# Four-block decoder kernel: who computes the layer norm that ends the mixture, VectorE or GpSimd

## The chip, the core and the metric

One core of one Trainium2 chip. The metric is the device time of one execution in microseconds (us). Engines are named as the profile names them: PE (TensorE, matrix products), DVE (VectorE), ACT (ScalarE), POOL (GpSimd), SP (SyncE, which only issues transfers here).

## What is computed

A decoder of two layers over x of 4 batches x 512 tokens x 128 channels. Each of its six steps is `x = layernorm(x + step(x))`. Cut to the two steps that matter here:

```python
# step 3: mixture of 16 experts, top 2, and a shared expert
hidden = silu(x @ gate) * (x @ up)            # per expert
x = layernorm(x + combine(hidden @ down) + shared(x))

# step 4: delta rule, 16 heads of 64
# W_t = W_(t-1) + beta_t (v_t - W_(t-1) k_t) k_t^T,   o_t = W_t q_t
x = layernorm(x + o @ Wout)

def layernorm(x): m = mean(x); v = mean((x - m)**2); return (x - m) / sqrt(v + 1e-5)
```

## The kernel before

x stays in SBUF as `X`, 16 tiles of 128 tokens x 128 channels, and is worked on in four blocks (one batch each, `xb(b)`, 128 partitions x 512 float32). Its transpose is `XT`. The stages are lettered: B is cross-attention, C the mixture, D the delta rule. Each engine runs its own instruction list in program order. `weave` mixes several generators into that list at build time: a `yield` is a point where another stream's instructions may come in. What stands in a list stays in that order whatever happens on the chip, and a wait at the head of an engine's list holds all that stands behind it.

Mixture (C). `c_experts_*` runs nine pairs of experts for each block: PE computes gate and up, ACT the silu (line 1318), DVE multiplies (lines 1335 and 1341, both with one operand in PSUM). Each block's turn also carries three side streams: the router of the next block (whose last DVE step, lines 1273 and 1275, writes `c_CT`, which PE needs before it can weight the next block's experts), the down projection of the block before, and that block's norm. `c_down_vector` adds the four down-projected tiles into `X` (line 1361) and then calls `normalize(..., "xr_C", fine=True)`: a sum per token (line 191), the mean (193), `x - mean` in place (197), the square into the one scratch tile `sq` (200), its sum (204), the variance (207), an inverse root by bit trick and three Newton steps in instructions of four elements per partition (lines 174, 176, 180, 165), and the product `x * root` (213), which raises `xr_C`. PE then transposes the block (`turn_tensor`, line 221). The norms of blocks 0, 1 and 2 run inside the turns of blocks 1, 2 and 3; that of block 3 runs later, in `c_last_vector`.

Already during the turns of blocks 2 and 3, the keys of the delta rule are made ready (`d_rows_*`, `d_turn_*`, with an inverse root of their own on tiles `d_z*`, and line 1600, which scales the keys `d_KV`).

Delta rule (D). The tokens are cut in chunks, and each chunk needs the inverse of a triangular matrix. There are eight such jobs m, each worth half the heads of one batch. `d_blocks_vector` (line 1638, two transposes) hands a job to GpSimd, `d_inverse_gpsimd` does it in 62 dependent instructions (lines 1709 and 1712), `d_back_vector` (line 1646, two transposes) and `d_back_scalar` bring it back as `d_XE`. PE multiplies with `d_XE` first in `corner`, then ACT negates (`d_NW`), DVE transposes a tile (`d_X`, line 1908), and PE runs `fold`. In `c_order`, the call `run(back(lane, 0))` stands right behind the mixture's weave: on DVE, all of block 3's adds and norm, the next job's transposes and everything of stage D stand behind its wait for the inverse of job 0.

GpSimd's list around the change: `d_clear_gpsimd` (a memset); `d_split_gpsimd` (line 1461, low halves of three weight matrices, each waiting for ACT); then the eight inverses; then four bias additions of the last stage.

Of the kernel before, what the change touches and what calls it, by code (L numbers as in the profile page):

```python
# [10 lines left out]
ALU = mybir.AluOpType  # L11
ACT = mybir.ActivationFunctionType
AX = mybir.AxisListType.X

NB, T, D, TC = 4, 512, 128, 154
# [13 lines left out]
    "f_lt": ("a_mz", 1), "f_lg": ("a_vz", 4), "f_oh": ("a_out", 4), "f_ctp": ("a_add", 4), "f_m": ("a_on", 16),  # L29
    "f_bm": ("a_oc", 16), "f_xm": ("a_pv", 64),  # L30
    "d_inv": ("a_ws", 4), "d_x1": ("b_kv", 6), "d_btm": ("b_kt", 6), "xr_E": ("xr_A", 4), "xr_F": ("xr_B", 4), "f_wh": ("d_wh", 3),
}


# [28 lines left out]
def run(gen):  # L63
    for _ in gen:
        pass


def bc(a, n):
    return a.unsqueeze(2).broadcast_to([a.shape[0], a.shape[1], n])
# [56 lines left out]
def build(nc, io, phases=6):  # L126
    with ExitStack() as ctx:
        sems = {}

        def sem(name):  # L130
            name = SHARED.get(name, (name, 0))[0]
            if name not in sems:
                sems[name] = ctx.enter_context(nc.semaphore(name))
            return sems[name]
# [3 lines left out]
        def at(name, shape, dt, word):  # L138
            return nc.alloc_sbuf_tensor_at(name, shape, dt, offset=SB0 + 4 * word)
# [6 lines left out]
        sq = at("sq", [128, 4, 128], F32, 4416)  # L146
        st = at("st", [128, 14, 4], F32, 4928)
# [4 lines left out]
        def xb(b):  # L152
            return X[:, 4 * b:4 * b + 4, :]
# [10 lines left out]
        def stt(e, out, a, s, b, op0, op1):  # L164
            return e.scalar_tensor_tensor(out=out, in0=a, scalar=s, in1=b, op0=op0, op1=op1)  # L165
# [4 lines left out]
        def rsqrt_steps(v, x, y, a, b):  # L170

            e = v.e
            v.wait_own()
            e.tensor_scalar(a.bitcast(I32), x.bitcast(I32), 1, None, ALU.logical_shift_right).then_inc(*v.step())
            v.wait_own()
            e.tensor_scalar(y.bitcast(I32), a.bitcast(I32), -1.0, float(MAGIC), ALU.mult, ALU.add).then_inc(*v.step())
            for k in range(3):
                yield
                v.wait_own()
                e.tensor_tensor(a, y, y, ALU.mult).then_inc(*v.step())  # L180
                v.wait_own()
                stt(e, b, a, -0.5, x, ALU.mult, ALU.mult).then_inc(*v.step())
                yield
                v.wait_own()
                stt(e, y, b, 1.5, y, ALU.add, ALU.mult).then_inc(*v.step())

        def normalize(v, x, eps, done=None, out=None, k=0, fine=False):

            e = v.e
            out = x if out is None else out  # L190
            e.tensor_reduce(st[:, k, :], x, AX, ALU.add).then_inc(*v.step())  # L191
            v.wait_own()
            e.tensor_scalar(st[:, k + 1, :], st[:, k, :], 1.0 / D, None, ALU.mult).then_inc(*v.step())
            if fine:
                yield
            v.wait_own()
            e.tensor_tensor(out, x, bc(st[:, k + 1, :], D), ALU.subtract).then_inc(*v.step())  # L197
            yield
            v.wait_own()
            e.tensor_tensor(sq[:], out, out, ALU.mult).then_inc(*v.step())  # L200
            if fine:
                yield
            v.wait_own()
            e.tensor_reduce(st[:, k + 2, :], sq[:], AX, ALU.add).then_inc(*v.step())
            yield
            v.wait_own()
            e.tensor_scalar(st[:, k + 3, :], st[:, k + 2, :], 1.0 / D, eps, ALU.mult, ALU.add).then_inc(*v.step())
            for _ in rsqrt_steps(v, st[:, k + 3, :], st[:, k + 4, :], st[:, k + 5, :], st[:, k + 6, :]):
                if fine:
                    yield  # L210
            yield
            v.wait_own()
            last = e.tensor_tensor(out, out, bc(st[:, k + 4, :], D), ALU.mult)  # L213
            if done:
                last.then_inc(sem(done), 1)
            else:
                last.then_inc(*v.step())
# [381 lines left out]
        def a_gpsimd(p):  # L599
            a_clear_gpsimd(p)  # L600
            for G in range(NG):
                a_row_gpsimd(p, G)
                if G in (0, 1, 4, 8):
                    a_split_gpsimd(p, (0, 1, 4, 8).index(G))
                if G % 4 == 2:
                    a_bias_gpsimd(p, G // 4)
# [530 lines left out]
        def b_gpsimd(p):  # L1137
            for u in range(NU):
                for s in range(11):
                    b_low_gpsimd(p, u, s)  # L1140
# [215 lines left out]
        def c_down_vector(v, b):  # L1356
            v.wait_ge("xr_B", b + 1)
            v.wait_ge("xt_B", b + 1)
            for n in range(4 * b, 4 * b + 4):
                v.wait_ge("c_dm", n + 1)  # L1360
                v.e.tensor_tensor(X[:, n, :], X[:, n, :], PS[:, bank["cd", n], 0:128], ALU.add).then_inc(sem("c_add"), 1)
                if n % 4 < 3:
                    yield
            v.wait_ge("c_add", 4 * b + 4)
            yield from normalize(v, xb(b), 1e-5, "xr_C", fine=True)

        def c_order(lane, route, experts, tail, rows, turn, last, blocks, back, split, parts):

# [81 lines left out]
        def d_clear_gpsimd(p):  # L1450

            p.wait_ge("b_sc", 11 * NU)
            p.wait_ge("b_mt", 16 * NU)
            p.wait_ge("b_r", 96 * NU)
            p.wait_ge("b_mr", 16 * NU)
            p.e.memset(d_XB, 0.0).then_inc(sem("d_zv"), 1)

        def d_split_gpsimd(p):
            for k, (w, f) in enumerate(((d_wk, d_fk), (d_wq, d_fq), (d_wv, d_fv))):
                p.wait_ge("d_wh", k + 1)  # L1460
                p.e.tensor_tensor(w[:, 1], f, w[:, 0], ALU.subtract).then_inc(sem("d_wl"), 1)
# [237 lines left out]
        def d_inverse_gpsimd(p, m):  # L1699
            e, G, XI = p.e, d_G[m % 2], d_XI[m % 2]  # L1700
            p.wait_ge(f"d_gr{m % 2}", 16 * (m // 2 + 1))
            p.wait_ge("d_gt", 2 * m + 2)
            for t in range(31, 0, -1):
                n = 32 - t
                tm = d_tmp[:, 0:t * n].rearrange("p (s t) -> p s t", s=t)
                a = G[:, t, 0:t].unsqueeze(2).broadcast_to([128, t, n])
                x = XI[:, t, t:32].unsqueeze(1).broadcast_to([128, t, n])
                p.wait_own()
                e.tensor_tensor(tm, a, x, ALU.mult).then_inc(*p.step())  # L1709
                p.wait_own()  # L1710
                z = XI[:, 0:t, t:32]
                last = e.tensor_tensor(z, z, tm, ALU.subtract)  # L1712
                if t > 1:
                    last.then_inc(*p.step())
            last.then_inc(sem("d_inv"), 1)
# [360 lines left out]
        def c_last_vector(v):  # L2076
            end = c_down_vector(v, NB - 1)
            for _ in range(3):
                next(end)
            yield from end  # L2080
# [433 lines left out]
        def none(lane, *_):  # L2514
            return iter(())
# [3 lines left out]
        @block.tensor  # L2519
        def _(e):  # L2520
            t = Lane(e, sem, "pe")
            a_tensor(t)
            b_tensor(t)
            if phases == 2:
                run(b_tail_tensor(t))
                return
            c_order(t, c_route_tensor, c_experts_tensor, b_tail_tensor(t), lambda t, m: d_rows_tensor(t, m, ring),
                    lambda t, m: d_turn_tensor(t, m, ring), c_down_tensor, lambda t: later(3, ()), none, lambda t: later(3, ()), lambda t, b: later(2, ()))
            hidden = f_hidden_tensor(t, 0)
            d_order(t, d_chain_tensor, d_prep_tensor, lambda t, m: d_keys(t, d_rows_tensor, d_turn_tensor, m, ringD),  # L2530
                    lambda t, m: d_rows_tensor(t, m, ringD), lambda t, m: d_turn_tensor(t, m, ringD), d_late_tensor, e_first_tensor,
                    e_attend_tensor, none, c_last_tensor, none, none, lambda t, b: f_route_tensor(t, b, ringD), hidden, none)
            f_start_tensor(t)
            f_order(t, f_hidden_tensor, hidden, f_route_tensor, none, f_late_tensor)
# [33 lines left out]
        @block.gpsimd  # L2568
        def _(e):
            p = Lane(e, sem, "pool")  # L2570
            a_gpsimd(p)
            b_gpsimd(p)
            if phases == 2:
                return
            d_clear_gpsimd(p)
            d_split_gpsimd(p)
            for m in range(NH):
                d_inverse_gpsimd(p, m)
            for b in range(NB):
                f_bias_gpsimd(p, b)  # L2580
# [124 lines left out]
```

## Time and profile before

| | us |
|---|---|
| median of 3 runs | 1770.7 (1767.85 to 1774.16) |
| the profiled execution | 1774.49 |
| its span in the profile | 1772.7 |
| norms of mixture blocks 0, 1, 2 on DVE (sum to product) | 1010.80 to 1027.42, 1054.52 to 1072.70, 1106.12 to 1122.13 |
| inverses of jobs 0 and 1 on POOL | 1085.05 to 1124.65, 1146.14 to 1184.58 |

All times inside the kernel count from the start of the span. A row of a timeline gives start, length, engine, line, operation, output <- inputs and, in brackets, how long the engine had been idle and what released it. A line number can be that of a helper.

### The profile page before, as it was taken

To read this page: it belongs to the slowest core of one execution; us is meant where nothing else is said; L and a number is where in the kernel's file an instruction comes from. 1 tells how busy PE (TensorE), PEld (TensorE's weight loads), DVE (VectorE), ACT (ScalarE), POOL (GpSimd) and SP (SyncE) were. 2 spreads that over 40 slices of the span, in tenths; PEclk is the share of its full clock that TensorE was granted. 3 is DMA by queue.
4 is the path that set the end of the run, shared out by engine and by line. 5 is a ranking of instruction groups with operands and counts; after the bars stand their busy time and mean duration, and the time that the engine had idled before them with its cause. 6 is when DMAs were issued, how large, how long until landed. Compare 5 with 4: busy or idle time off the path is not lost.

```text
span 1772.7 us, 41545 instructions
## 1 busy us (share of the span) xinstructions
PE 1526.5 (86%) x17916; PEld 800.5 (45%) x17916; DVE 1214.3 (68%) x2341; ACT 915.1 (52%) x1269; POOL 681.6 (38%) x716
## 2 busy tenths in 40 slices
PE   5887877789999999999988988788989899898985
PEld 1222222333334333433423544677777788665542
DVE  6889875777774776667545667766866775565776
ACT  1676654566774777577574333355445444333220
POOL 1111000355564655466473104467855567000000
PEclk9999998899999999999998998799999998879998
DMA  4000002223322222223120100000000001100000
GB/s 149 1 1 1 1 1 81 85 70 88 93 81 58 81 70 85 54 86 102 38 69 14 62 1 13 13 15 4 16 15 16 15 4 35 50 2 1 1 13 12
DMA packets 32407, 70.63 MB, mean 40 GB/s; under 512 B 5328, under 2 KB 7056, under 8 KB 31968
## 3 DMA queue, kind: packets, MB, share of 16 engines
q1 hardware_dynamic: 32224, 67.98, 13.1%
q8 instruction: 141, 2.31, 0.5%
q14 instruction: 42, 0.34, 0.1%
HBM read 47.45 MB, written 20.51 MB: 38 GB/s over the span
## 4 chain that ended last, share of the span: by engine, by line
PE 58%; DVE 28%; ACT 6%; issue 5%; DMA 1%; POOL 1%; SPq 0%; DVEq 0%; ACTq 0%; POOLq 0%
PE ps L159 56%; DVE a_MX L401 4%; DVE b_mx L834 3%; PE ps L221 1%; PE ps L1523 1%; DVE st L165 1%; DVE b_VL L781 1%; DVE sq L200 1%; DVE d_KV L1600 1%; POOL b_EL L906 1%; ACT d_L L162 1%; DVE st L191 1%; DMA b_M<-s_xq 1%; DVE X L197 1%; DVE d_zb L165 1%
## 5 line engine op out<-in xcount | busy, mean ns | idle before, releaser
L906 POOL TENSOR_TENSOR b_EL<-b_X,b_EH 128x1024 f16<-128x1024 f32 x160 | 341.2, 2133 | 309.0 <-ACT b_EH L162 309.0
L834 DVE TENSOR_REDUCE b_mx<-ps 128x2 f32<-128x666 f32 x256 | 216.9, 847 | 99.9 <-PE ps L159 99.7
L888 ACT ACTIVATE b_X<-ps 128x1024 f32<-128x1024 f32 x160 | 163.8, 1024 | 133.9 <-PE ps L159 132.9
L1709 POOL TENSOR_TENSOR d_tmp<-d_G,d_XI 128x31 f32<-128x31 f32 (+15 forms) x248 | 128.9, 520 | 193.2 <-DVE d_G L1638 174.4
L162 ACT ACTIVATE b_EH<-b_X 128x1024 f16<-128x1024 f32 x160 | 169.1, 1057 | 27.9 <-PE ps L159 16.7
L159 PE MATMUL ps<-b_M,b_S 128*128 128x512 f16 (+1 forms) x768 | 177.1, 384 | 2.0 <-ACT b_X L888 2.0
L438 ACT ACTIVATE a_E<-ps 128x1024 f32<-128x1024 f32 x128 | 131.3, 1025 | 91.0 <-PE ps L159 90.5
L401 DVE TENSOR_REDUCE a_MX<-ps 128x2 f16<-128x1024 f32 x128 | 155.4, 1226 | 29.1 <-PE ps L159 27.7
L1712 POOL TENSOR_TENSOR d_XI<-d_XI,d_tmp 128x31 f32<-128x31 f32 (+15 forms) x248 | 141.0, 569 | 19.5
L159 PE MATMUL ps<-b_Hk,b_Hq 64*128 64x333 f16 x512 | 82.6, 319 | 40.4 <-DVE b_mx L834 36.1
L420 POOL TENSOR_TENSOR a_QS<-a_QS,a_MR 128x512 f16<-128x512 f16 x16 | 18.5, 1157 | 234.7 <-ACT a_MR L162 234.7
L159 PEld LDWEIGHTS ps<-b_Hk,b_Hq 64*128 64x128 f16 x512 | 24.6, 93 | 164.1 <-DVE b_mx L834 139.5
L159 PEld LDWEIGHTS ps<-b_M,b_S 128*128 128x128 f16 (+1 forms) x768 | 55.5, 97 | 77.2 <-issue 25.2
L2446 POOL TENSOR_TENSOR f_Y<-X,f_bo 128x512 f32<-128x512 f32 x4 | 6.1, 1536 | 215.5 <-DVE X L213 112.8
L159 PE MATMUL ps<-f_XM,f_Wh 128*128 128x512 f16 x256 | 78.1, 387 | 0.0
L159 PE MATMUL ps<-a_QS,a_KS 32*128 32x512 f16 x256 | 52.2, 405 | 29.8 <-DVE a_MX L401 28.7
L162 ACT ACTIVATE d_UW<-ps 128x512 f32<-128x512 f32 x64 | 38.2, 597 | 68.9 <-PE ps L159 68.9
L159 PE MATMUL ps<-a_E,a_VA 128*32 128x512 f32 x512 | 72.9, 643 | 0.3
L159 PE MATMUL ps<-d_KV,d_XE 64*64 64x128 f32 x1024 | 72.7, 291 | 0.1
L159 PE MATMUL ps<-b_EH,b_VH 128*64 128x512 f16 x320 | 65.5, 406 | 5.0 <-POOL b_EL L906 2.5
L1318 ACT ACTIVATE c_SG<-ps 128x512 f32<-128x512 f32 x36 | 21.5, 597 | 88.1 <-PE ps L159 86.5
L159 PEld LDWEIGHTS ps<-d_KV,d_XE 64*64 64x64 f32 x1024 | 62.2, 145 | 5.2 <-issue 4.2
(322 smaller groups left out, 3324.2 us busy)
## 6 DMA issues: line engine op xcount, KB each, us to landing
b_S<-s_xk SPq DMA_DIRECT2D x48, 336.0 KB, 6.3
b_M<-s_xq SPq DMA_DIRECT2D x48, 256.0 KB, 5.0
s_xk<-b_Hk SPq DMA_DIRECT2D x16, 336.0 KB, 2.2
s_xk<-b_Lk SPq DMA_DIRECT2D x16, 336.0 KB, 2.5
s_xq<-b_Hq SPq DMA_DIRECT2D x16, 256.0 KB, 2.0
s_xq<-b_Lq SPq DMA_DIRECT2D x16, 256.0 KB, 2.0
d_XI<-eye SPq DMA_DIRECT2D x8, 512.0 KB, 3.8
f_w<-f_w SPq DMA_DIRECT2D x1, 2048.0 KB, 8.1
```

Of the source, the lines that this page charges most:

```text
L159: return e.matmul(out, lhsT, rhs, start=start, stop=stop, skip_group_check=True)
L162: return e.activation(out, a, ACT.Copy)
L165: return e.scalar_tensor_tensor(out=out, in0=a, scalar=s, in1=b, op0=op0, op1=op1)
L401: v.e.tensor_reduce(out, PS[:, bk:bk + 2, :], AX, ALU.max).then_inc(sem("a_mx"), 1)
L420: p.e.tensor_tensor(a_QS[G % 4], a_QS[G % 4], a_MR[G % 2], ALU.add).then_inc(sem("a_q2"), 1)
L438: a.e.activation(a_E[c][:, 2 * hp:2 * hp + 2, :], PS[:, bk:bk + 2, :], ACT.Exp, scale=float(D) ** -0.5).then_inc(sem("a_ex"), 1)
L834: v.e.tensor_reduce(out, PS[:, bk:bk + 2, 0:333], AX, ALU.max).then_inc(sem("b_mx"), 1)
L888: a.e.activation(b_X[k % 2], PS[:, bk:bk + 2, :], ACT.Exp, scale=0.125).then_inc(sem("b_ex"), 1)
L906: last = p.e.tensor_tensor(b_EL[k % 6], b_X[k % 2], b_EH[k % 6], ALU.subtract)
L1318: a.e.activation(c_SG[n % 3], PS[:, bank["cgu", b, p], :], ACT.Silu).then_inc(sem("c_sl"), 1)
L1709: e.tensor_tensor(tm, a, x, ALU.mult).then_inc(*p.step())
L1712: last = e.tensor_tensor(z, z, tm, ALU.subtract)
```

## The change

For blocks 0, 1 and 2, DVE keeps the two sums, the mean, the variance and the roots. The difference, the square and the last product go to GpSimd. Three semaphores pass the work: `c_nm` (mean ready), `c_nq` (squares ready), `c_ny` (root ready, by a new copy of four elements per partition). Block 3 is as before. DVE's first wait, for `c_nq`, stands ahead of the second sum. GpSimd's list becomes: memset; difference and square of block 0; the weight splits; product of block 0; block 1; block 2; and then the inverses.

```diff
             v.wait_ge("c_add", 4 * b + 4)
-            yield from normalize(v, xb(b), 1e-5, "xr_C", fine=True)
+            v.wait_ge("xr_C", b)
+            if b == NB - 1:
+                yield from normalize(v, xb(b), 1e-5, "xr_C", fine=True)
+            else:
+                yield from c_norm_vector(v, b)
+
+        def c_norm_vector(v, b):
+            e = v.e
+            e.tensor_reduce(st[:, 0, :], xb(b), AX, ALU.add).then_inc(*v.step())
+            v.wait_own()
+            e.tensor_scalar(st[:, 1, :], st[:, 0, :], 1.0 / D, None, ALU.mult).then_inc(sem("c_nm"), 1)
+            yield
+            yield
+            yield
+            v.wait_ge("c_nq", b + 1)
+            e.tensor_reduce(st[:, 2, :], sq[:], AX, ALU.add).then_inc(*v.step())
+            yield
+            v.wait_own()
+            e.tensor_scalar(st[:, 3, :], st[:, 2, :], 1.0 / D, 1e-5, ALU.mult, ALU.add).then_inc(*v.step())
+            for _ in rsqrt_steps(v, st[:, 3, :], st[:, 4, :], st[:, 5, :], st[:, 6, :]):
+                yield
+            v.wait_own()
+            e.tensor_copy(st[:, 7, :], st[:, 4, :]).then_inc(sem("c_ny"), 1)
+            yield
+
+        def c_norm_gpsimd(p, b):
+            e, x = p.e, xb(b)
+            p.wait_ge("c_nm", b + 1)
+            p.wait_ge("xt_B", b + 1)
+            e.tensor_tensor(x, x, bc(st[:, 1, :], D), ALU.subtract).then_inc(*p.step())
+            p.wait_own()
+            e.tensor_tensor(sq[:], x, x, ALU.mult).then_inc(sem("c_nq"), 1)
+            yield
+            p.wait_ge("c_ny", b + 1)
+            p.wait_ge("c_nq", b + 1)
+            e.tensor_tensor(x, x, bc(st[:, 7, :], D), ALU.mult).then_inc(sem("xr_C"), 1)
@@ gpsimd
             d_clear_gpsimd(p)
+            first = c_norm_gpsimd(p, 0)
+            next(first)
             d_split_gpsimd(p)
+            run(first)
+            for b in range(1, NB - 1):
+                run(c_norm_gpsimd(p, b))
             for m in range(NH):
                 d_inverse_gpsimd(p, m)
```

(The three semaphores are also given shared numbers in a table at the top of the file.)

## Rows read from the trace of the kernel before

**Rows 1.** Page of the profile: busy time of each engine over the span.

```profile
PE 1526.5 (86%) x17916; PEld 800.5 (45%) x17916; DVE 1214.3 (68%) x2341; ACT 915.1 (52%) x1269; POOL 681.6 (38%) x716
```

**Rows 2.** Busy by stretch: length, PE, PEld, DVE, ACT, POOL, granted clock, DMA share, GB/s.

```profile
1080.00:1122.00 42.00, 34.55 (x143) 18.24 (x141) 36.06 (x64) 14.41 (x24) 32.64 (x56) 0.92 0.04 13
1122.00:1163.00 41.00, 35.31 (x748) 31.48 (x749) 21.12 (x50) 15.63 (x25) 16.85 (x36) 0.83 0.05 15
...
1144.50:1148.00 3.50, 3.42 (x124) 3.39 (x128) 1.76 (x7) 1.18 (x2) 1.47 (x6) 0.50 0.02 7
```

**Rows 3.** Timeline of PE (start us, length us, ..., idle before it <-releaser), mixture to delta rule.

```profile
1021.58 2.07 PE L159 MATMUL ps<-XT,c_gt 128*128 128x512 f32 x2 [4.30 <-DVE c_CT L1275]
...
1066.60 2.08 PE L159 MATMUL ps<-XT,c_gt 128*128 128x512 f32 x2 [7.20 <-DVE c_CT L1275]
...
1106.14 1.61 PE L159 MATMUL ps<-XT,c_gt 128*128 128x512 f32 x2 [1.70 <-DVE X L1361]
...
1139.22 1.20 PE L159 MATMUL ps<-d_XE,d_L 32*32 32x32 f32 x64
...
1144.58 1.92 PE L159 MATMUL ps<-d_NW,d_X 32*32 32x32 f32 x64 [2.92 <-DVE d_X L1908]
```

**Rows 4.** Timeline of POOL (GpSimd), from the weight splits to the second inverse.

```profile
1014.36 2.21 POOL L1461 TENSOR_TENSOR d_wv<-d_fv,d_wv 128x1024 f16<-128x1024 f32 x1 [0.33 <-ACT d_wv L162]
1085.05 0.24 POOL L1709 TENSOR_TENSOR d_tmp<-d_G,d_XI 128x31 f32<-128x31 f32 x1 [68.48 <-DVE d_G L1638]
...
1124.40 0.25 POOL L1712 TENSOR_TENSOR d_XI<-d_XI,d_tmp 128x31 f32<-128x31 f32 x1
1146.14 0.24 POOL L1709 TENSOR_TENSOR d_tmp<-d_G,d_XI 128x31 f32<-128x31 f32 x1 [21.48 <-DVE d_G L1638]
...
1184.33 0.25 POOL L1712 TENSOR_TENSOR d_XI<-d_XI,d_tmp 128x31 f32<-128x31 f32 x1
```

**Rows 5.** Timeline of DVE (VectorE), norm of block 0.

```profile
1011.52 0.44 DVE L193 TENSOR_SCALAR st<-st 128x4 f32<-128x4 f32 x1
...
1014.62 2.50 DVE L200 TENSOR_TENSOR sq<-X 128x512 f32<-128x512 f32 x1
...
1020.85 0.68 DVE L1275 TENSOR_TENSOR c_CT<-ps,c_CT 16x512 f16<-16x512 f32 x1
```

**Rows 6.** Timeline of DVE, norm of block 2.

```profile
1121.44 0.69 DVE L213 TENSOR_TENSOR X<-X,st 128x512 f32<-128x512 f32 x1
```

**Rows 7.** Groups of DVE by line and form (xcount | busy us, mean ns), 1053 to 1069.

```profile
L165 DVE SCALAR_TENSOR_TENSOR d_zy<-d_zb,d_zy 128x64 f32<-128x64 f32 x3 | 0.7, 223 | 0.1
...
L1600 DVE TENSOR_TENSOR d_KV<-d_KV,d_f 128x512 f32<-128x512 f32 x4 | 2.6, 686 | 0.0
```

**Rows 8.** The same groups, 1093 to 1110, where POOL inverts.

```profile
L165 DVE SCALAR_TENSOR_TENSOR d_zy<-d_zb,d_zy 128x64 f32<-128x64 f32 x3 | 2.1, 696 | 0.1
...
L1600 DVE TENSOR_TENSOR d_KV<-d_KV,d_f 128x512 f32<-128x512 f32 x4 | 3.9, 1026 | 0.0
```

**Rows 9.** Groups of POOL by form, whole span: float32 tiles of 128x512.

```profile
L2446 POOL TENSOR_TENSOR f_Y<-X,f_bo 128x512 f32<-128x512 f32 x4 | 6.1, 1536 | 215.5 <-DVE X L213 112.8 <-PE ps L159 102.7
L315 POOL TENSOR_TENSOR X<-X,a_bo 128x512 f32<-128x512 f32 x4 | 5.1, 1269 | 0.0
```

**Rows 10.** Timeline of DVE, from the first inverse's use to the fold.

```profile
1129.03 2.28 DVE L1646 STREAM_TRANSPOSE d_XE<-d_XI 128x512 f32<-128x512 f32 x2
...
1141.51 1.15 DVE L1638 STREAM_TRANSPOSE d_G<-d_L 128x512 f32<-128x512 f32 x1 [0.94 <-ACT d_L L162]
...
1143.77 0.70 DVE L1908 STREAM_TRANSPOSE d_X<-d_XE 128x512 f32<-128x512 f32 x1
```

**Rows 11.** Timeline of ACT (ScalarE) in the same stretch.

```profile
1131.35 2.12 ACT L162 ACTIVATE d_XE<-d_XE 32x1024 f32<-32x1024 f32 x2 [5.63 <-DVE d_XE L1646]
1138.73 0.60 ACT L1840 ACTIVATE d_QT<-ps 128x512 f32<-128x512 f32 x1 [5.26 <-PE ps L159]
1139.36 2.12 ACT L162 ACTIVATE d_L<-d_L 32x1024 f32<-32x1024 f32 x2
```

More of the change, by code:

```diff
@@ L31 @@
     "d_inv": ("a_ws", 4), "d_x1": ("b_kv", 6), "d_btm": ("b_kt", 6), "xr_E": ("xr_A", 4), "xr_F": ("xr_B", 4), "f_wh": ("d_wh", 3),
+    "c_nm": ("b_pm", 144), "c_nq": ("b_lo", 144), "c_ny": ("b_pc", 144),
 }
```

## The prediction

> **What bounds the kernel now.** I read first the busy times: PE is busy 86% of the span, POOL 38% [rows 1]. POOL as a whole has room, so the question is only where the moved steps stand in its list. Second, the stretches around the change [rows 2]. From 1080 to 1122 DVE is busy 36.06 of 42 us and PE 34.55, and from 1122 to 1163 DVE is busy 21.12 of 41. So DVE is the tight engine in the second half of the mixture and has air right behind it. Third, PE's timeline says where DVE sets the time: PE sits idle 4.30 us ahead of 1021.58 and 7.20 us ahead of 1066.60, both until DVE has written `c_CT`, then 1.70 us ahead of 1106.14 for the last add into `X`, and 2.92 us ahead of the first fold at 1144.58 for `d_X` [rows 3]. Fourth, POOL's timeline: the inverse of job 0 runs from 1085.05 to 1124.65, that of job 1 from 1146.14 to 1184.58, each following at once on DVE's `d_G` [rows 4]. DVE takes up the first one at 1129.03 [rows 10], 4.4 us after it ended. These four views give the shape of the case: the change frees DVE where it is tight, and puts the end of block 2's norm ahead of an inverse that today runs beside it.
>
> **Block 0.** Today the mean is there at 1011.96, and the square takes 2.50 us from 1014.62 [rows 5]. It is long because the last weight split, which began at 1014.36 and took 2.21, had to end first (1016.57) [rows 4]. A 128x512 float32 pass costs POOL 1.27 us (four bias additions) to 1.54 (four others) [rows 9]. I take 1.27: those ran with nothing waited for before them, as these will. The mean comes at about 1011.7, as no split is in its way. Difference and square end at 1014.4, so DVE's second sum starts 2.7 us sooner than the end of today's square, 1017.12. But the three splits, 2.2 us each, now begin at 1014.5 and end at 1021. Behind that sum and one expert pair DVE is at 1016.4 with the small steps of the root, all with their operands in SBUF. Where POOL works without a gap, such a step takes as long as POOL's instruction: 696 ns against 223 [rows 7, 8]. So each remaining split lets one through: they end at 1021.5 in place of about 1020.1, and `c_CT`, which follows and for which PE waits, ends at 1022.8 in place of 1021.53 [rows 3, 5]. Cost +1.3 us. Bounds: -2.5, if the small steps slip in between splits, to +1.5. The Trainium skill ("SBUF — State Buffer", section "Who interferes with whom") has this as a rule: the pair of ports that VectorE and GpSimd share is locked for a whole instruction, and whoever asks later stands still. By that rule the square's 2.50 us is a wait of 1.95 and 0.55 of work, and the trace agrees. It speaks against moving passes to GpSimd beside small VectorE steps, and it is the rule behind the +1.3.
>
> **Block 1.** No split is near. DVE drops two passes of 0.69 us ahead of `c_CT`. POOL's two passes, 2.5 us together, fall on the start of the keys' root chain and hold two of its steps, up to 1.3 us. Net -0.3, bounds -1.4 and +1.3. The product on POOL instead of DVE ends about 1 us later. Its taker is the transpose of the block one turn later, and the same hand-over in block 2 lies at `c_last`, so both are covered. Blocks 0 and 1 together: +1.0 us.
>
> **Block 2: the relief.** The inverse of job 0 leaves this stretch. DVE's eleven instructions of the keys' root chain lose 0.47 us each (696 to 223 ns), at most 5.2; the four scalings of the keys 0.34 each (1026 to 686), 1.4 [rows 7, 8]; three passes move away, at least 2.1, less 0.2 for the new copy. That is 8.5 us of DVE work. PE can't use all of it: in this stretch it is idle for 42 - 34.55 = 7.45 us, and its granted clock is 0.92, worth another us or two [rows 2]. I take 8 us of relief. Bounds: 4, if PE or the wait for POOL's squares keeps half, to 9.5, PE's idle time and clock together.
>
> **Block 2: the price.** POOL's list is in order, and all of block 2's norm now stands ahead of the first inverse. The root is ready when the product starts today, 1121.44 [rows 6], less 8, plus 1.0, plus 0.1 for the copy: 1114.5. The product takes 1.3, so the inverse of job 0 begins at 1115.9 and not at 1085.05. It takes 39.60 us beside busy DVE, 38.44 for job 1 [rows 4]. DVE will stand still, so 38.4: end at 1154.3, which is 29.6 later than 1124.65.
>
> **What is late next.** DVE's list holds its wait for the inverse ahead of block 3's adds, its norm and the hand-over of job 1. PE does block 3's down projections, which need nothing of that, and then stops at `corner`. From the inverse's end to the fold every step now follows on the one before: two transposes 2.28 (one row for both) [rows 10], the copies of `d_XE` 2.12, one copy of `d_QT` 0.60, the copies of `d_L` 2.12 [rows 11], and from their end (1141.48) to the fold at 1144.58 another 3.1, in which DVE runs the rest up to `d_X` [rows 3, 10]. With hand-overs 10.4. DVE's adds and first passes of block 3 fit beside these 4.8 us of ACT. Today that way has 1144.58 - 1124.65 = 19.9 us, so 9.5 of the delay are absorbed. The fold moves to 1164.7: +20.1 us. The inverse of job 1 waits for `d_G`, of which one half stands ahead of `d_X` and the other right behind, so it moves by the same amount, and from there on all four engines are late together. I find nothing later that isn't: the loads of stage D are behind the same marks.
>
> **The sum.** +1.0 - 8 + 0.1 + 1.3 + 0.1 for the norm's end against the start of the product (1121.44), 1115.9; + 38.4 + 10.4 = 1164.7; less 1144.58 = +20.1. Against the profiled execution's 1774.5 that is 1794.6. That execution lies 3.8 above the median of the runs, so against the median, 1770.7, it is 1790.8: 1791. With the bounds (relief 4 to 9.5, blocks 0 and 1 -3.5 to +1.5, the pass 1.27 to 1.54, the inverse 38.4 to 39.6) the forecast's own range is +15 to +26: 1786 to 1797.
>
> **Rivals.** (1) PE's clock. Today PE has `corner` in hand at 1139.22 [rows 3]; 8 us sooner its work ahead of it is done, and `d_XE` comes at 1154.3 + 4.5, so PE rests from about 1131 to 1159. After only 2.92 us of idleness it ran at half clock, 1.2 GHz, from 1144.5 to 1148 [rows 2, 3]. If a longer rest keeps it at half clock for some 14 us of work more, 7 us come on top: 1798. Against it: the way to the fold is bound by ACT and DVE, and today's fold is run at half clock too. The Trainium skill ("TensorE: Matmul & The Clock Gate") says that an array that rested starts again at 1.2 GHz; here that holds for either kernel, so it changes the chance of this rival little. (2) The relief doesn't come, so that the change doesn't do what it says: DVE waits at `c_nq` for POOL's squares and for the ports, as it waited today for its own passes. Price 6 to 8 us: 1798. For it: the square of block 0, 2.50 us [rows 5]; against it: by block 2 there is nothing else in POOL's list. (3) Stage D takes some of the delay back, as PE is idle 14% of the time from 1122 to 1163 [rows 2]; a third to all but 5 us of the delay gone is 1776 to 1784. Against it: those idle times are waits for steps that are late as well. (4) The other side: the delay of the inverse is hidden. This needs the inverse to end by 1144.58 - 10.4 = 1134.2, that is the inverse to start by 1095.8, ahead of block 2's norm. Then only the relief is left, +1.0 - 8: 1764. The list of POOL forbids it, unless I misread where the norm of block 2 stands.
>
> **How the numbers follow.** Chances: forecast 0.70, (1) 0.12, (2) 0.08, (3) 0.07, (4) 0.03. The range 1781 to 1799 holds the forecast whole, most of (1) and (2) and some of (3). What a measurement can tell from no change is 0.3%, 5.3 us: faster is below 1765.4, slower above 1776.0. Faster: (4), 0.03. Same: the low edge of (3), 0.02. Slower: 0.95.
>
> **What would show it.** POOL: first inverse from about 1116 to 1154, and its idle time before it no longer ended by `d_G` but by the norm's product. DVE: idle some 25 us ahead of line 1646, released by POOL, and PE idle about as long ahead of the first `corner`. From 1092 to 1114 the keys' root steps at about 0.22 us. `c_CT` of block 0's turn near 1023, and its PE wait above 4.3 us. Wrong would be: a wait at `corner` under 15 us, small steps still at 0.6 us, or a last stretch, from fold to end, whose length has changed by more than 3 us.

## The result, and the profile after

The changed kernel takes 1791.07 us (median of 4 runs, 1786.92 to 1796.1). The kernel before took 1771.22 beside it. The ratio is 1.011, with a 95% interval of 1.0082 to 1.0138: 20 us slower. The profiled execution took 1788.91 us, and its span is on the page:

```profile
span 1786.9 us, 41557 instructions
...
PE 1515.1 (85%) x17916; PEld 793.3 (44%) x17916; DVE 1203.0 (67%) x2335; ACT 914.5 (51%) x1269; POOL 687.6 (38%) x725
```

[Rows 1] answers to it: POOL gained 6 us of work and DVE lost 11, and the kernel got slower all the same. The added line of code shifts the lines of helpers by one (159 is now 160) and those of the delta rule by 36 (1709 is now 1745).

POOL's timeline (columns as in [rows 4]) shows the new order of its list. `1395`, `1397` and `1401` are difference, square and product, `1497` a weight split:

```profile
1012.99 1.04 POOL L1395 TENSOR_TENSOR X<-X,st 128x512 f32<-128x512 f32 x1 [64.61 <-DVE st L1376]
1014.11 1.04 POOL L1397 TENSOR_TENSOR sq<-X 128x512 f32<-128x512 f32 x1
1015.11 2.13 POOL L1497 TENSOR_TENSOR d_wk<-d_fk,d_wk 128x1024 f16<-128x1024 f32 x1
1017.20 2.12 POOL L1497 TENSOR_TENSOR d_wq<-d_fq,d_wq 128x1024 f16<-128x1024 f32 x1
1019.27 2.12 POOL L1497 TENSOR_TENSOR d_wv<-d_fv,d_wv 128x1024 f16<-128x1024 f32 x1
...
1104.04 1.04 POOL L1395 TENSOR_TENSOR X<-X,st 128x512 f32<-128x512 f32 x1 [29.28 <-DVE st L1376]
1105.16 1.04 POOL L1397 TENSOR_TENSOR sq<-X 128x512 f32<-128x512 f32 x1
...
1114.81 1.04 POOL L1401 TENSOR_TENSOR X<-X,st 128x512 f32<-128x512 f32 x1 [8.61 <-DVE st L1388]
1115.81 0.24 POOL L1745 TENSOR_TENSOR d_tmp<-d_G,d_XI 128x31 f32<-128x31 f32 x1
...
1152.07 0.25 POOL L1748 TENSOR_TENSOR d_XI<-d_XI,d_tmp 128x31 f32<-128x31 f32 x1
1165.15 0.24 POOL L1745 TENSOR_TENSOR d_tmp<-d_G,d_XI 128x31 f32<-128x31 f32 x1 [12.82 <-DVE d_G L1674]
```

The reader is to see three things. A pass takes 1.04 us. The first inverse (1115.81 to 1152.32) follows on the product of block 2 without a gap, where it ran from 1085.05 to 1124.65 [rows 4]. The second starts at 1165.15, 19.0 us later than 1146.14.

DVE, norms and the first use of the inverse:

```profile
1017.39 1.95 DVE L1384 TENSOR_SCALAR st<-st 128x4 f32<-128x4 f32 x1
1019.37 2.04 DVE L175 TENSOR_SCALAR st<-st 128x4 int32<-128x4 int32 x1
...
1022.84 0.68 DVE L1276 TENSOR_TENSOR c_CT<-ps,c_CT 16x512 f16<-16x512 f32 x1
...
1105.20 2.15 DVE L1636 TENSOR_TENSOR d_KV<-d_KV,d_f 128x512 f32<-128x512 f32 x2
...
1107.88 0.67 DVE L1381 TENSOR_REDUCE st<-sq 128x4 f32<-128x512 f32 x1
...
1114.56 0.17 DVE L1388 COPY st<-st 128x4 f32<-128x4 f32 x1
...
1152.43 2.24 DVE L1682 STREAM_TRANSPOSE d_XE<-d_XI 128x512 f32<-128x512 f32 x2 [32.09 <-POOL d_XI L1748]
1154.57 0.84 DVE L1362 TENSOR_TENSOR X<-X,ps 128x128 f32<-128x128 f32 x4
```

DVE stands still for 32.09 us, released by POOL; in the kernel before it took the inverse up at 1129.03 with no wait [rows 10]. The first two rows are steps of four elements per partition that took 1.95 and 2.04 us, one beside each of the last two splits. PE, in the same two places:

```profile
1023.57 2.08 PE L160 MATMUL ps<-XT,c_gt 128*128 128x512 f32 x2 [5.06 <-DVE c_CT L1276]
...
1068.07 2.07 PE L160 MATMUL ps<-XT,c_gt 128*128 128x512 f32 x2 [5.80 <-DVE c_CT L1276]
...
1154.87 1.46 PE L160 MATMUL ps<-d_wv,d_XS 128*128 128x256 f16 x6 [27.65 <-DVE X L1362]
1156.13 1.48 PE L160 MATMUL ps<-d_XS,d_wq 128*128 128x512 f16 x3
...
1163.56 1.20 PE L160 MATMUL ps<-d_NW,d_X 32*32 32x32 f32 x64 [2.48 <-DVE d_X L1944]
```

PE waits 5.06 us for `c_CT` of block 0's turn (4.30 before) and 5.80 for that of block 1 (7.20 before) [rows 3]. Then it stands still for 27.65 us, and the fold comes at 1163.56 in place of 1144.58. The same two stretches as in [rows 2], with the first one cut where the product starts (length, PE, PEld, DVE, ACT, POOL, granted clock, DMA share, GB/s):

```profile
1080.00:1114.00 34.00, 32.20 (x143) 17.64 (x144) 26.74 (x61) 13.70 (x23) 2.08 (x2) 1.00 0.06 17
1122.00:1163.00 41.00, 11.42 (x133) 8.84 (x131) 8.40 (x17) 7.08 (x9) 26.56 (x49) 0.67 0.04 13
```

In the first stretch PE is busy 95% of the time at full clock, where it was 82% at 0.92 from 1080 to 1122. In the second, PE is busy 11.42 us of 41, against 35.31. One stretch got faster and one stood still.

**A common ruler.** Single executions start the stage some us apart (1010 to 1020 us from the start of the span). So all kernels are measured from the same start below: the last of the four adds of block 0 into `X` (line 1361 or 1362) to the start of the first fold. This way is called the ruler. The kernel before needs 134.10 us (1010.48 to 1144.58), the changed one 151.86 (1011.70 to 1163.56). That is +17.8. It is read in one execution of each kernel, so differences of a us or two on it need a row that explains them. From the fold to the end of the span they need 628.1 and 623.3, and all further kernels 620 to 624, so the kernel before had a slow tail of 4 us or more in its profiled execution. The spans differ by 1.2 + 17.8 - 4.8 = 14.2 us, the medians by 19.9.

### The profile page after: what moved, and what is told of

It is laid out like the page before. It is cut to its first block, busy times and chain, and to the rows that moved or that the text cites. A ratio compares the mean times of both kernels' runs of the same rounds, so it can differ in the third digit from the quotient of the medians.

```text
span 1786.9 us, 41557 instructions
## 1 busy us (share of the span) xinstructions
PE 1515.1 (85%) x17916; PEld 793.3 (44%) x17916; DVE 1203.0 (67%) x2335; ACT 914.5 (51%) x1269; POOL 687.6 (38%) x725
## 4 chain that ended last, share of the span: by engine, by line
PE 57%; DVE 27%; ACT 6%; issue 5%; POOL 3%; DMA 1%; SPq 0%; DVEq 0%; ACTq 0%; POOLq 0%
PE ps L160 55%; DVE a_MX L402 4%; DVE b_mx L835 3%; PE ps L222 1%; POOL d_XI L1748 1%; DVE st L166 1%; POOL d_tmp L1745 1%; DVE b_VL L782 1%; PE ps L1559 1%; POOL b_EL L907 1%; ACT d_L L163 1%; DVE d_XE L1682 1%; DVE sq L201 1%; DVE st L192 1%; DVE a_KS L166 1%
## 5 line engine op out<-in xcount | busy, mean ns | idle before, releaser
L439 ACT ACTIVATE a_E<-ps 128x1024 f32<-128x1024 f32 x128 | 131.2, 1025 | 91.6 <-PE ps L160 91.2
L421 POOL TENSOR_TENSOR a_QS<-a_QS,a_MR 128x512 f16<-128x512 f16 x16 | 18.5, 1155 | 235.2 <-ACT a_MR L163 235.2
```

The lines of the kernel that those rows point to most:

```text
L421: p.e.tensor_tensor(a_QS[G % 4], a_QS[G % 4], a_MR[G % 2], ALU.add).then_inc(sem("a_q2"), 1)
L439: a.e.activation(a_E[c][:, 2 * hp:2 * hp + 2, :], PS[:, bk:bk + 2, :], ACT.Exp, scale=float(D) ** -0.5).then_inc(sem("a_ex"), 1)
```

## The experiments

All times in us. Inverse, fold and the way from add to fold are from the profiled execution of each kernel. Each ratio is against the kernel before as it was timed beside that kernel: its median was 1771.2 beside the changed kernel, 1770.0 beside e1 to e7 and 1770.2 beside e8.

| kernel | median | ratio to before, 95% | inverse of job 0 | fold | add to fold |
|---|---|---|---|---|---|
| before | 1771.2 | | 1085.05 to 1124.65 | 1144.58 | 134.1 |
| changed | 1791.1 | 1.0110 [1.0082, 1.0138] | 1115.81 to 1152.32 | 1163.56 | 151.9 |
| e1_block2_back | 1768.0 | 0.9992 [0.9967, 1.0016] | 1089.17 to 1128.71 | 1145.92 | 131.2 |
| e2_block2_only | 1787.8 | 1.0113 [1.0069, 1.0157] | 1118.09 to 1154.67 | 1165.90 | 151.2 |
| e3_hold_inverse | 1787.0 | 1.0116 [1.0071, 1.0160] | 1115.26 to 1151.86 | 1163.10 | 152.2 |
| e4_splits_later | 1765.6 | 0.9982 [0.9958, 1.0006] | 1083.56 to 1123.20 | 1140.41 | 125.5 |
| e4_again | 1764.7 | 0.9969 [0.9951, 0.9988] | 1084.68 to 1124.37 | 1141.13 | 124.5 |
| e5_before_splits_later | 1768.3 | 0.9981 [0.9961, 1.0000] | 1090.10 to 1129.72 | 1149.64 | 132.5 |
| e6_interleaved | 1765.2 | 0.9962 [0.9940, 0.9985] | 1087.05 to 1129.13 | 1145.59 | 126.8 |
| e7_back_later | 1792.0 | 1.0106 [1.0077, 1.0135] | 1123.83 to 1160.33 | 1173.63 | 153.6 |
| e8_back_behind_adds | 1793.2 | 1.0125 [1.0073, 1.0176] | 1122.41 to 1159.72 | 1169.20 | 150.3 |

The theory is that of the prediction: the whole loss is the late start of the inverse, and it is late because block 2's norm stands ahead of it in POOL's list.

**e1: block 2 back on DVE.** Blocks 0 and 1 stay as in the change.

```diff
-            if b == NB - 1:
+            if b >= NB - 2:
                 yield from normalize(v, xb(b), 1e-5, "xr_C", fine=True)
@@ gpsimd
-            for b in range(1, NB - 1):
+            for b in range(1, NB - 2):
                 run(c_norm_gpsimd(p, b))
```

> The change for blocks 0 and 1 alone; block 2's norm is on VectorE again, so GpSimd's list has nothing but the splits and two norms ahead of the first inverse. Theory (order of GpSimd's list): the inverse of job 0 starts at about 1086 again and the time is that of the kernel before, 1771 us, give or take 3. Rival (the passes themselves, the shared port and VectorE's waits for GpSimd): the loss of 20 us falls on the three norms in about equal parts, so two thirds of it stay: 1784 us.

**e2: block 2 alone on POOL.** The mirror image: blocks 0 and 1 are normalized by DVE.

```diff
-            if b == NB - 1:
+            if b != NB - 2:
                 yield from normalize(v, xb(b), 1e-5, "xr_C", fine=True)
@@ gpsimd
-            first = c_norm_gpsimd(p, 0)
-            next(first)
             d_split_gpsimd(p)
-            run(first)
-            for b in range(1, NB - 1):
-                run(c_norm_gpsimd(p, b))
+            run(c_norm_gpsimd(p, NB - 2))
```

(Not shown: the waits for `c_nm`, `c_nq` and `c_ny` ask for 1, as only one block raises them.)

> The change for block 2 alone. Theory (order of the list): nearly the whole loss, 1789 to 1791 us, inverse of job 0 from about 1115 to 1151. Rival (the passes themselves): a third of the loss, 1778 us.

**e3: the kernel before, with the inverse held.** No pass is moved. POOL only waits for the end of block 2's norm, which DVE computes.

```diff
             d_clear_gpsimd(p)
             d_split_gpsimd(p)
+            p.wait_ge("xr_C", NB - 1)
             for m in range(NH):
                 d_inverse_gpsimd(p, m)
```

> The kernel before, no pass moved; only GpSimd waits for the end of block 2's norm (on VectorE) before it begins the first inverse. Theory (order of the list): the whole loss without any pass on GpSimd. VectorE gets the relief from the port (about 6 us in 1092 to 1122) but keeps its three passes, so the inverse starts at about 1116 and the time is 1791 us, 1788 to 1794. Rival (the passes themselves): 1771 us, or 6 us less, 1765, as the small steps are no longer held.

The first and the last instruction of the inverse on POOL; e1, then e2, then e3 with its fold on PE:

```profile
1089.17 0.24 POOL L1745 TENSOR_TENSOR d_tmp<-d_G,d_XI 128x31 f32<-128x31 f32 x1 [11.32 <-DVE d_G L1674]
...
1128.46 0.25 POOL L1748 TENSOR_TENSOR d_XI<-d_XI,d_tmp 128x31 f32<-128x31 f32 x1
```

```profile
1118.09 0.24 POOL L1745 TENSOR_TENSOR d_tmp<-d_G,d_XI 128x31 f32<-128x31 f32 x1
...
1154.42 0.25 POOL L1748 TENSOR_TENSOR d_XI<-d_XI,d_tmp 128x31 f32<-128x31 f32 x1
```

```profile
1115.26 0.24 POOL L1709 TENSOR_TENSOR d_tmp<-d_G,d_XI 128x31 f32<-128x31 f32 x1 [98.27 <-DVE X L213]
...
1151.61 0.25 POOL L1712 TENSOR_TENSOR d_XI<-d_XI,d_tmp 128x31 f32<-128x31 f32 x1
...
1163.10 1.20 PE L159 MATMUL ps<-d_NW,d_X 32*32 32x32 f32 x64 [2.39 <-DVE d_X L1908]
```

All three came out by the theory: e1 at 1768.0 us, the low edge of 1771 give or take 3, and e2 at 1787.8 and e3 at 1787.0, about 1 us under their ranges and 17.8 and 17.0 us over the kernel before. The whole loss sits in block 2: e2 shows it without blocks 0 and 1, and e1 is without it. e3 goes further. Its inverse runs from 1115.26 to 1151.86 and its fold is at 1163.10, each within 0.6 us of the changed kernel's, with none of the work moved. So the moved work itself adds nothing to the loss that can be seen; what costs is the place of the inverse behind the end of that norm.

e3 also says where the relief comes from. Counted from the common start, block 2's root was ready at 110.96 in the kernel before (start of its product), at 102.86 in the changed one (start of the copy for POOL) and at 103.60 in e3 (start of the product, the row below). So 7.4 of the 8.1 us of gain come from the absence of the inverse beside DVE, and the moved passes bring under 1 us.

```profile
1114.49 0.69 DVE L213 TENSOR_TENSOR X<-X,st 128x512 f32<-128x512 f32 x1
```

**e4: e1, with the splits behind block 0's norm.** e1 still has POOL's splits beside the small steps of block 0's root. Here they follow on the product. The edit is shown against e1.

```diff
-            first = c_norm_gpsimd(p, 0)
-            next(first)
-            d_split_gpsimd(p)
-            run(first)
+            run(c_norm_gpsimd(p, 0))
+            d_split_gpsimd(p)
```

> As e1_block2_back, and the three weight splits stand behind block 0's whole norm on GpSimd (about 1029 to 1036; their first use by TensorE is near 1043). Theory: in the kernel with the change two small steps of VectorE waited 1.95 and 2.04 us for splits, ahead of c_CT, for which TensorE waits. Both waits go, c_CT of block 0's turn ends 3.7 us sooner, and the time is 3 to 4 us under e1_block2_back: 1767 to 1768 us. Rival: the two waits are covered by TensorE's work of that turn, or the splits are late where they now stand: same as e1_block2_back or slower.

e4 came to 1765.6 us, 2.4 under e1, where 3 to 4 were expected. The same kernel was timed a second time, as e4_again, beside e5, e6 and e7. (The add from which its text counts is the last of the four, the start of the ruler.)

> The kernel of e4_splits_later once more, to learn its ratio to the kernel before more closely. From the third down-projected add of block 0's turn to the fold of the first delta-rule job the traces show 134.1 us before, 131.2 in e1_block2_back and 125.4 in e4_splits_later. If that 8.6 us is real and nothing later gives it back: 1762 to 1766 us, ratio 0.995 to 0.998. If it is given back later: 1770 us.

**e5: the kernel before, with its splits held likewise.** It tells whether e4's gain is that of the splits alone.

```diff
             d_clear_gpsimd(p)
+            p.wait_ge("xr_C", 1)
             d_split_gpsimd(p)
```

> The kernel before, all norms on VectorE, only the three weight splits wait for the end of block 0's norm. It prices the port alone. Theory: block 0's mean, difference and square lose 0.3, 0.3 and 1.8 us of standing still, TensorE's wait for c_CT falls from 4.3 to about 2 us, and if the granted clock then stays up, its next expert pair runs at full speed, another 1 to 2 us. 3 to 4 us under the kernel before: 1766 to 1768 us. Rival (moving the passes is what gained in e4_splits_later): 1770 to 1771 us.

PE's first expert pair after `c_CT` of block 0's turn, with the wait ahead of it: e1 (with its fold), then e4 (with its first split on POOL), then e5 (with the square on DVE).

```profile
1026.63 2.08 PE L160 MATMUL ps<-XT,c_gt 128*128 128x512 f32 x2 [5.07 <-DVE c_CT L1276]
...
1145.92 1.20 PE L160 MATMUL ps<-d_NW,d_X 32*32 32x32 f32 x64 [2.92 <-DVE d_X L1944]
```

```profile
1023.17 1.13 PE L160 MATMUL ps<-XT,c_gt 128*128 128x512 f32 x2 [1.41 <-DVE c_CT L1276]
...
1028.10 2.13 POOL L1497 TENSOR_TENSOR d_wk<-d_fk,d_wk 128x1024 f16<-128x1024 f32 x1
```

```profile
1021.02 0.69 DVE L200 TENSOR_TENSOR sq<-X 128x512 f32<-128x512 f32 x1
...
1026.18 2.07 PE L159 MATMUL ps<-XT,c_gt 128*128 128x512 f32 x2 [2.21 <-DVE c_CT L1275]
```

In e4 `c_CT` ends 8.2 us after the common start, in e1 11.8, and PE waits 1.41 us in place of 5.07. The pair behind it takes 1.13 us in place of 2.08: full clock in place of half. That is where e4 gets most of what it has beyond the 3.7 us of the shorter wait: from `c_CT` to block 1's last add it takes 30.8 us (30.6 in e4_again) against 32.9. Add to fold is 125.5 (e4) and 124.5 (e4_again) against 131.2. In e5 the square takes 0.69 us in place of 2.50 [rows 5], so nothing holds DVE. The wait is 2.21 us, and the pair is at half clock still. e5's shorter way is 1.6 us. The Trainium skill ("TensorE: Matmul & The Clock Gate", section "Part 1: The HAM clock gate") says that an idle array falls back to half rate; these rows agree, with 1.41 us of idleness that left the clock up and 2.21 that did not. The level isn't a function of the wait alone. Later in the mixture, PE waited 1.70 us in the kernel before, and the clock fell within the pair behind it (1.61 us at 1106.14 [rows 3]); 1.71 us in e4 left it at full (1.12 us). And the same 2.92 us of waiting before the fold left it at half in the kernel before (1.92 us [rows 3]) and at full in e1 (1.20).

The times say less than the ruler, which is one execution of each. Of the two timings of e4, the first can't be told from the kernel before (0.9982, up to 1.0006) and the second, 1764.7 us as expected, is faster by 0.12 to 0.49%. e5 is faster by 0 to 0.39%: 1.7 us in the medians, where 3 to 4 were expected. e4's lead over e1, 2.4 us in the medians, isn't clear of the spread either. e4 leads e5 by 7 to 8 us on the ruler and by 3.6 us in the medians, with intervals that overlap. Of the lead on the ruler, 3.6 to 4.4 us lie behind `c_CT` of block 1's turn, where of the moved work only block 1's product lies (0.7 us of DVE). At least 1.2 of these are PE's clock alone: its 72 products for block 3's down projection took 8.30 us in e4 and in e1 (granted clock 1.00), 9.51 in e5 (0.87) and 9.64 in the kernel before (0.85). So e4_again is faster than the kernel before; how its gain divides between the splits' place and the two moved norms isn't shown.

**e6: all three norms on POOL, block 2's inside the inverse.** The splits are as in e4. Block 2's difference and square stand at one point of the 62 steps of the first inverse, its product at a later one.

```diff
+            run(c_norm_gpsimd(p, 0))
+            d_split_gpsimd(p)
+            run(c_norm_gpsimd(p, 1))
             for m in range(NH):
-                d_inverse_gpsimd(p, m)
+                d_inverse_gpsimd(p, m, c_norm_gpsimd(p, 2) if m == 0 else None)
@@ d_inverse_gpsimd, in the loop over t
                 n = 32 - t
+                if norm and t == 14:
+                    next(norm)
+                if norm and t == 5:
+                    run(norm)
```

> All of the change, with two differences in GpSimd's list: the splits stand behind block 0's norm, and block 2's difference and square stand inside the inverse of job 0 (after 17 of its 31 double steps), its product five double steps from the end. Theory (order of the list): the inverse starts near 1084, ends some 3.5 us later than in e4_splits_later and still before VectorE asks for it, so the 20 us are not paid, and VectorE saves block 2's three passes (2.8 us there, with the port held): 1 to 2.5 us under e4_splits_later, 1763 us. Rival: VectorE's waits for GpSimd's squares eat that or more, as GpSimd's own steps stand ahead of them: 1767 us.

POOL (difference, product, last step of the inverse) and DVE's first use of it:

```profile
1109.06 1.04 POOL L1395 TENSOR_TENSOR X<-X,st 128x512 f32<-128x512 f32 x1 [0.66 <-DVE st L1376]
...
1124.01 1.04 POOL L1401 TENSOR_TENSOR X<-X,st 128x512 f32<-128x512 f32 x1
...
1128.88 0.25 POOL L1752 TENSOR_TENSOR d_XI<-d_XI,d_tmp 128x31 f32<-128x31 f32 x1
```

```profile
1130.20 2.27 DVE L1682 STREAM_TRANSPOSE d_XE<-d_XI 128x512 f32<-128x512 f32 x2
```

The inverse lasts 42.1 us with the three passes in it, from 1087.05 to 1129.13, and DVE comes for it at 1130.20 without a wait. With all three norms moved and the list in another order, the loss of the change is gone: 0.9962. The time, 1765.2 us, falls between the theory (1763) and the rival (1767). It can't be told from e4_again (0.9969), and on the ruler e6 needs 126.8 us against 125.5 and 124.5. The rows say why block 2's relief doesn't come while the inverse stands beside DVE: two of the key scalings took 2.14 us together beside steps of the inverse, and the two beside POOL's square took 2.57, against 1.29 where POOL is silent.

**e7 and e8: DVE's wait moved down.** The rival of e3's reading: the late inverse would cost little if DVE didn't stand in front of it with block 3's adds and norm behind its wait. Both take the changed kernel and put the two transposes of `back` into the weave of the next stretch, e7 at its head and e8 behind block 3's adds and first norm steps.

```diff
-            run(back(lane, 0))
@@ e7
-            weave((last_c(lane), 18), (prep(lane, 0), 17), (later(2, blocks(lane, 1)), 24))
+            weave((back(lane, 0), 20), (last_c(lane), 18), (prep(lane, 0), 17), (later(2, blocks(lane, 1)), 24))
@@ e8
+            weave((last_c(lane), 18), (prep(lane, 0), 17), (later(2, blocks(lane, 1)), 24), (later(8, back(lane, 0)), 52))
```

> The kernel with the change; the two transposes and copies that bring the inverse of job 0 back stand some steps later in the lists of VectorE and ScalarE, behind block 3's adds, the copies for job 1 and one product of the preparation, and just ahead of what needs them. It tests the step of the prediction on what is late next. Theory: the inverse still ends near 1152, TensorE now does the first values and queries before it, and from the inverse's end to the fold it takes 7 to 8 us and not 11.2: 3 to 4 us under the kernel with the change, 1787 us, most of the loss stays. Rival: the wait of VectorE in its own list is what costs, and the time comes within 8 us of the kernel before: under 1779 us.

> As e7_back_later was meant: the kernel with the change, and on VectorE the two transposes of the first inverse now stand behind block 3's adds, its first passes, the values of the preparation and half of job 1's hand-over, on ScalarE behind the copies for job 1. (In e7_back_later the first of the two transposes had stayed ahead of the adds, VectorE waited there all the same, and nothing was gained.) Theory: TensorE does values and queries during the inverse and stops at corner; from the inverse's end to the fold 7 to 8 us in place of 11.2, and job 1 starts some 8 us sooner after it. 3 to 6 us under the kernel with the change, 1785 to 1788 us: most of the loss is the inverse's late end, not what VectorE keeps behind its wait. Rival: under 1779 us.

PE at the end of its long wait, e7 and then e8:

```profile
1161.83 1.46 PE L160 MATMUL ps<-d_wv,d_XS 128*128 128x256 f16 x6 [26.59 <-DVE X L1362]
```

```profile
1165.02 1.92 PE L160 MATMUL ps<-d_XE,d_L 32*32 32x32 f32 x64 [29.25 <-ACT d_XE L163]
...
1169.20 1.92 PE L160 MATMUL ps<-d_NW,d_X 32*32 32x32 f32 x64
```

e7's edit didn't do what it was meant to: the weave put the first transpose ahead of the adds still, and PE waits at the same place (26.59 us, for `X`). It says nothing on the rival; its time, 1792.0 us, is that of the changed kernel. In e8 the adds come first, and PE does the work on the values and queries before its wait and stops at `corner`, where the prediction had it. From the end of the inverse (1159.72) to the fold it takes 9.5 us in place of 11.2. Yet `corner` and fold run at half clock (1.92 us each; 1.20 each in the changed kernel), and the inverse of job 2 begins 69.7 us after that of job 0 ended, against 70.6 in the changed kernel. Of the 1.8 us about 1 is left, and the kernel is not faster at all (1793.2, where 1785 to 1788 was expected). So the order on DVE is worth about 1 us of the 20 in these two executions, and nothing that the times show; the rest is the late inverse.

## Why the prediction was right

Direction, size and mechanism were right; 1790.8 was predicted, rounded to 1791. The terms, against the traces of the two kernels on the common ruler:

| step | predicted | measured |
|---|---|---|
| block 0, add to `c_CT` | +1.3 | +0.77 |
| block 1, add to `c_CT` | -0.3 | -0.70 |
| relief, `c_CT` of block 1 to block 2's root | -8 | -8.36 |
| pass and hand-overs | +1.5 | +1.25 |
| start of the inverse against the product's start before | -5.5 | -6.85 |
| inverse | 38.4 us | 36.5 us |
| its end to the fold | 10.4 us | 11.24 us |
| fold against before | +20.1 | +17.8 |

The first four measured terms add up to 0.19 us less than the start of the inverse shows; the stretch between `c_CT` of block 0 and block 1's last add, for which the prediction had no term, took that much longer.

The range has a slip. Its bounds for blocks 0 and 1 (-3.5 to +1.5) are not the sum of the two blocks' bounds, which is -3.9 to +2.8, and its low end, with the bounds as stated, is +14 and not +15. The measured time lies well inside either way.

**Block 0.** The rule was one small step of DVE per split, and the trace shows just that: 1.95 us at 1017.39, 2.04 at 1019.37. The splits don't hold everything: the sum at 1015.19 and the two expert products with an operand in PSUM at 1016.06 and 1016.78 took 0.69 us each beside them. The term was too high by 0.5: the two passes took 1.04 us each and not 1.27, and a split 2.12 and not 2.2, so the last split ended 9.7 us after the common start and not 10.5. The Trainium skill's rule on the shared ports ("SBUF — State Buffer", section "Who interferes with whom") is borne out by e4: without a split beside them the same way to `c_CT` is 3.7 us shorter. The square of the kernel before, read as 1.95 us of wait and 0.55 of work, took 0.69 alone in e5, so the wait was nearer 1.8.

**Block 1.** POOL's passes held one step of the keys' root (1.08 us at 1058.83), not two. The gain of 0.70 lies inside the bounds.

**Relief.** The size was right, and its division was not, so two errors cancelled. The prediction added root steps (5.2), scalings (1.4) and moved passes (about 2) to 8.5 and took 8: 6.6 for the missing inverse, the rest for the moved passes. The small steps did fall to 224 ns (223 and 696 in [rows 7, 8]). But e3 has no moved pass and gets 7.4. One reason is a term that the prediction left out: the inverse also held block 2's own passes, whose difference and square took 1.17 and 0.96 us in the kernel before and 0.68 and 0.69 in e3. The moved passes' 2 us of DVE work bring 0.7: two key scalings beside POOL's square took 2.15 us at 1105.20, against 1.28 in e3. That PE had little idle time left to use may be the rest; no run separates it. DVE did not wait at `c_nq` (the sum at 1107.88 follows at once), so the rival in which the relief doesn't come is refuted.

**The price.** The inverse began at 1115.81, 1115.9 predicted. That near agreement is in part chance: the changed kernel's execution came to the common start 1.2 us later, and on the ruler the inverse began 1.3 us sooner than predicted. The mis-sized term is its length. The prediction took the second inverse of the kernel before, 38.44 us, as the value without DVE beside it, but DVE was half busy there too [rows 2]. Alone it takes 36.5 (the changed kernel, e2 and e3: 36.5, 36.6, 36.6), and beside a busy DVE 39.5 to 39.7 (before, e1, e4, e5). On the ruler the sum was 2.3 us too large: 1.3 of it in the start of the inverse (the terms above), 1.9 in its length, less the 0.84 of the next step.

**From the inverse to the fold.** Here a step was wrong, and it cost only 0.84 us. The prediction let PE go on to `corner` and had it stop there. It stopped one item sooner, at the values (27.65 us, for `X`): the PSUM tiles that these need still held block 3's down projections, and their adds into `X` stand behind DVE's wait. At `corner` it then didn't wait at all. So values and queries ran after the pause and at half clock (1.46 and 1.48 us; 0.82 and 0.81 in e8, which did them before it), and ACT waited 0.9 us for the copy of `d_QT`. The prediction had seen what stands behind DVE's wait, and had not asked which buffers of PE's are held by it.

**Its own signs of being wrong.** It had named three. The small steps fell to 0.22 us, as it wanted. The other two came true by their letter. There is no wait of 15 us at `corner`, since the long wait stands one item ahead of it, and the stretch from fold to end changed by 4.8 us, more than the 3 allowed. The tail of the kernel before was the odd one (628.1 us; 619.7 to 623.8 in the ten others), so the second says something of that execution and not of the change.

**The other rivals.** Stage D takes next to nothing back: the inverse of job 1 starts 19.0 us later than before, that of job 2 18.5 (1222.95 against 1204.41), that of job 7 18.6 (1480.37 against 1461.79). Less the 1.2 us of the later start, these are 17.8, 17.3 and 17.4. After the long rest PE is at full clock again at the fold (1.20 us at 1163.56, 1.92 before [rows 3]), so the rival that kept it at half clock has no more than the 1 us above. PE worked at half clock for 2.9 us (values and queries) and was back at full at `corner` (1.20 us at 1158.64). The hidden delay is excluded by the list, as e3 (inverse held, loss there) and e6 (inverse not held, loss gone) show from both sides.

**Where the sum and the median meet.** The sum was +20.1, the ruler says +17.8, the medians +19.9. The medians' ratio allows +14.5 to +24.4, so both fit it. The predicted number came so close in part because the profiled execution of the kernel before was no typical one: its way after the fold was 4 us or more longer than in all others. Taking the 3.8 us between that execution and the median off the end, as the prediction did, was right in direction, but the agreement to 0.1 us is chance.

## What to carry to other kernels

When a step goes to an engine that is "38% busy", ask what stands behind it in that engine's list, not how much room the engine has: three passes of 1 us put a chain of 36 us behind them, and a wait at the same place (e3) cost as much. Such passes can be moved where nothing serial stands behind them (blocks 0 and 1) or be woven into the chain itself (e6); with the long weight splits moved away from DVE's small steps, the first gave 0.2 and 0.3% in two timings (e4), both together 0.4% (e6), which is at the edge of what can be told here, and e4 is the simpler. And a shorter wait of TensorE can pay twice, once as time and once as clock: in e4 3.7 us less of it made the way to block 1's last add 5.8 to 6.0 us shorter than in e1, of which the medians show 2.4, not clear of their spread.

## What the runs showed of the hardware

- A 128x512 float32 difference, square or product took GpSimd 1.04 us, and DVE 0.68 to 0.69 with nothing of GpSimd's beside it (e3). GpSimd took 1.27 and 1.54 for bias additions of that form [rows 9]; why these differ wasn't tried. The Trainium skill ("GPSIMD Engine Reference", section "3.1 Elementwise — side-by-side cycle accounting") gives a ratio of 1.96 to VectorE for longer rows; here it is 1.5.
- GpSimd pays for working beside DVE too: the 62 steps of an inverse took 36.5 to 36.6 us beside a mostly waiting DVE and 39.5 to 39.7 beside a busy one, 3 us or 8%.
- DVE's steps of four elements per partition (0.17 us) took 1.95 and 2.04 us beside 2.12 us instructions of GpSimd, one for each. A 128x512 sum took its usual 0.69 beside such an instruction.
- PE kept its full clock over 1.40 and 1.41 us of idleness (e4, e4_again, e6), and was at half after 2.21 (e5) and after 4.3 us and more at the same place. In between the length of the wait didn't decide it: after 1.70 and 1.71 us the expert pair took 1.12, 1.61 or 1.75 us, and after 2.92 us the fold took 1.20 (e1, e4_again), 1.40 (e4) or 1.92 us (the kernel before, e6).
